# Begin the loads of one-hot matrices on ScalarE instead of SyncE, and drop the last layer's store of node rows

## The reference, cut to what matters

```python
x = x @ encW + encb
ea = edge_attr @ eencW + eencb
x = _genconv(x, src, dst, ea, ...)            # layer 0
for i in range(1, L):                         # layers 1, 2, 3
    h = relu(_ln(x, normG[i], normB[i]))
    h = _genconv(h, src, dst, ea, ...)
    x = x + h
...
# _genconv: m = relu(x[src] + ea) + EPS; logits = m * t
#   mx = segment_max(logits, dst); e = exp(logits - mx[dst])
#   agg = segment_sum(m * e / denom[dst], dst); h = agg + x; then a two-matrix network per node
```

## Time and profile before

| what | value |
|---|---|
| median of 3 runs | 11808.61 us (11800.38 to 11816.48) |
| the profiled execution's own time | 11828.1 us |
| its span | 11826.3 us |
| granted TensorE clock, mean of the span | 0.694 of full speed |
| TensorE matmuls, busy share of the span | 49% |
| VectorE, ScalarE, GpSimd, busy share | 55%, 28%, 55% |
| 16 DMA engines, mean moved | 115 GB/s |
| one-hot loads | 312, of 625 KB each |

### The profile page before, as it was taken

One profiled execution on the slowest core, in us unless ns is written; L12 is line 12 of the kernel. 1 busy time (PEld: TensorE's weight loads), 2 busy tenths in 40 slices (PEclk: granted clock), 3 DMA queues, 4 the chain that ended last, 5 costly groups with the idle time before them and its releaser, 6 DMA issues. The chain is left out here.

```text
span 11826.3 us, 107787 instructions
## 1 busy us (share of the span) xinstructions
PE 5802.2 (49%) x31762; PEld 4077.1 (34%) x31762; DVE 6551.7 (55%) x8055; ACT 3327.1 (28%) x4948; POOL 6522.0 (55%) x6157
## 2 busy tenths in 40 slices
PE   2333333343444444444444444444444447888887
PEld 2222222232333333333333333333333334444443
DVE  5666666664444444544444445444444457998897
ACT  1333333342333333333333333333223232111110
POOL 5455455535444444454544444544444446888887
PEclk6666666666666666666666666666666668999998
DMA  5344344333333333333333333333333334555555
GB/s 155 125 137 138 123 140 132 130 109 103 118 117 117 117 117 117 102 97 116 119 118 118 117 118 106 95 117 118 117 117 117 117 112 94 99 97 99 96 94 86
DMA packets 840467, 1354.58 MB, mean 115 GB/s; under 512 B 499934, under 2 KB 556476, under 8 KB 838730
## 3 DMA queue, kind: packets, MB, share of 16 engines
q1 hardware_dynamic: 523832, 1135.94, 27.5%
q0 software_dynamic: 312640, 214.30, 12.9%
q10 hardware_dynamic: 3916, 3.40, 0.1%
HBM read 806.66 MB, written 546.46 MB: 114 GB/s over the span
## 5 line engine op out<-in xcount | busy, mean ns | idle before, releaser
L826 POOL DMA_INDIRECT xg<-h_tab,idx x4656 | 4461.7, 958 | 4370.0 <-DVE idx L1159 2909.3
L917 PE MATMUL turn<-hb,hot 125*128 125x192 bf16 x12480 | 1872.5, 295 | 3018.0 <-issue 2977.7
L917 PEld LDWEIGHTS turn<-hb,hot 125*128 125x128 fp8e4 x12480 | 1310.6, 114 | 3571.7 <-issue 3536.0
L1159 DVE COPY idx<-idx_full 128x24 int32 x208 | 36.6, 176 | 3526.7 <-ACT zl L1035 3526.7
L933 PE MATMUL turn<-ident,sums 128*128 128x128 f32 x5184 | 1073.7, 375 | 1533.8 <-ACT st_all L1050 1140.4
L1524 POOL DMA_INDIRECT acc<-vm,tgt x1026 | 1602.9, 1562 | 341.2 <-issue 288.1
L933 PEld LDWEIGHTS turn<-ident,sums 128*128 128x128 f32 x5184 | 878.0, 222 | 1676.3 <-ACT st_all L1050 1243.6
L1066 ACT ACTIVATE hx<-turn 128x384 bf16<-128x384 f32 x156 | 76.4, 490 | 3600.9 <-PE turn L917 3553.1
L1050 ACT ACTIVATE st_all<-turn 128x512 f32<-128x512 f32 (+1 forms) x1344 | 752.3, 577 | 698.7 <-PE turn L933 321.0
L1166 DVE TENSOR_TENSOR_SCAN rx<-rp,carry,zl 128x1536 f32<-128x1536 bf16 (+1 forms) x224 | 739.9, 3303 | 360.1 <-ACT zl L1035 343.1
L1597 PE MATMUL zl<-spreadz,lo_hot 128*128 128x512 f32 x1620 | 765.5, 609 | 95.2 <-DVE spreadz L1773 95.2
(11 more groups left out here) (277 smaller groups left out, 7413.2 us busy)
## 6 DMA issues: line engine op xcount, KB each, us to landing
sums<-st_all SPq DMA_DIRECT2D x208, 1536.0 KB
hot<-hot_tab SPq DMA_DIRECT2D x312, 625.0 KB
ea<-feat SPq DMA_DIRECT2D x158, 768.0 KB
srcB<-src_flat SPq DMA_DIRECT2D x108, 768.0 KB
rp<-run_pen SPq DMA_DIRECT2D x210, 384.2 KB
xg<-h_tab,idx POOLq DMA_INDIRECT x4656
hot_tab<-hot SPq DMA_DIRECT2D x104, 625.0 KB
run_head<-zeros SPq DMA_DIRECT2D x216, 192.0 KB
```

The costliest lines, as they stand in the source:

```text
L826: g_.indirect_dma_start(xg[b][:, k, h, :], None, h_tab[:, :], bass.IndirectOffsetOnAxis(ap=idx[b][:, h, k:k + 1] if small is None else idx ...
L917: ins = pe.matmul(picked[:, :, n % 2, :], hot[n][0:PN, t_, :], hb[0:PN, t_, :, :], start=t_ == 0, stop=t_ == NT - 1, skip_group_check=True)
```

## The change

The loads of one-hot matrices for window w + 1 are begun by ScalarE, right behind its copy `hx<-turn` of window w, both at once. SyncE begins only the pair of window 0 of each layer. On ScalarE the last step of the loop over pairs of windows is written out behind the loop, since its second window is the last full one and has none after it to load for. Apart from this, SyncE no longer stores the node rows after the last layer, and waits for the semaphore of the computed rows instead of the one of the stored rows.

```diff
-                    def load_hot(l, w):
+                    def load_hot(l):
                         for n in range(HOT[l]):
-                            if isinstance(w, int) and w == 0 and n == 0:
+                            if n == 0:
                                 sp.wait_ge(hot_out, out_count(l, 0))
-                            if not (isinstance(w, int) and w == 0):
-                                sp.wait_ge(hot_ps, ps_count(l, w - 1, n))
-                            sp.dma_start(hot_words[n][0:PN, :], hot_tab[n][w]).then_inc(hot_in, 16)
+                            sp.dma_start(hot_words[n][0:PN, :], hot_tab[n][0]).then_inc(hot_in, 16)
...
-                        for w in range(2):
-                            load_hot(l, w)
+                        load_hot(l)
...
-                                load_hot(l, 2 * i + 2 + b)
...
-                        for k in range(NCH):
+                        for k in range(NCH if l + 1 < L else 0):
                             sp.wait_ge(h_ok, NCH * l + k + 1)
                             store_nodes(k)
...
-                    sp.wait_ge(tab_out, 16 * NCH * L + 16)
+                    sp.wait_ge(tab_out, 16 * NCH * (L - 1) + 16)
+                    sp.wait_ge(h_ok, NCH * L)
...
                             a.activation(hx[b][:, r, :, taken, :], part[:, :, taken, :], ACT.Copy).then_inc(hx_sb, 1)
+                        if not (isinstance(w, int) and w == FULLW - 1):
+                            for n in range(HOT[l]):
+                                a.dma_start(hot_words[n][0:PN, :], hot_tab[n][w + 1]).then_inc(hot_in, 16)
...
-                        with a.Fori(0, FULL_PAIRS - 1) as i:
+                        def pair(i):
...
+                        with a.Fori(0, FULL_PAIRS - 2) as i:
+                            pair(i)
+                        pair(FULL_PAIRS - 2)
```

## The result

The changed kernel takes 11952.04 us (median of 4 runs, 11944.34 to 11960.04) against 11807.31 us of before: ratio 1.0122, 95% interval 1.0105 to 1.014. That is 145 us slower, where 101 us were forecast. The two profiled executions lie 125 us apart (spans of 11826.3 and 11951.6 us), since that of before was 19.5 us above the median of its runs.

A forecast was written before the change was run, and what follows sets the result against it. The prediction took a serial ring through GpSimd's gathers, TensorE, ScalarE and VectorE in layers 1 to 3 to bound the kernel. Terms 99 + 0 + 3 - 1.7 gave +100 us; 11808.6 + 101 = 11910 us, range 11790 to 12250.

The forecast's parts named there:

- The main term: On ScalarE between `hx` and `keep`: issuing two DMAs adds 0.65 us a window, 153 times, +99 us.
- Two signs: In the changed profile: the ring at 43.2 to 43.4 us, about 21 matmuls of `select` left when TensorE resumes.
- the ring: Layers 1 to 3, each window: index copy, gathers, `select`, `hx`, `keep`, `u`, `zl`, next index copy; 42.64 us.
- The rival by the Trainium skill's rule: On ScalarE the issue hides wholly beside copy `hx`, so no difference: 11810 us; chance 0.08.
- the "0" for the later loads: `select` starts some 2 us later, but the count of matmuls done before TensorE stops stays: 0 us.
- The first rival: In `select`, fewer matmuls precede TensorE's stop with the later start: +1.0 us a window, 12060 us; chance 0.17.
- A: Theory of the follow-up runs: two costs, 0.65 us of ScalarE issue and 0.36 us of `select` matmuls from later loads.
- B: Theory of the follow-up runs: the DMA issue on ScalarE is the whole cost.
- The faster case: In `select`, up to 7 more matmuls precede TensorE's stop: -0.53 us a window, 11730 us; chance 0.10.
- Layer beginnings: Window 1 of a layer: both loads begin together, `select` starts some 4 us later; 1 us each, +3 us.
- The last store: Behind the last layer: SyncE no longer issues the store or waits for its landing, -1.7 us.

The follow-up runs named there:

- SyncE late: The kernel of before without the last store, SyncE waiting for copy `hx` before either load: 8775.32 us, ratio 1.0001; in a later session 8774.04 us, 0.9998.
- a1_after: The changed kernel run again with nothing altered: 11951.76 us against 11831.31 us of before, ratio 1.0105.
- `keep` first: The changed kernel with `keep` of the next window put ahead of the wait for `select`: 8774.34 us, ratio to before 0.9997.

## Why the prediction was right, and where it was off

**The main term held.** It said that `keep` would go from 0.39 to about 1.04 us behind `hx`. Over all regular windows it went from 0.45 to 1.10 us (+0.65), the first gather from 7.80 to 8.45 us behind `hx` (+0.65): 153 x 0.65 = 99 us of the 145. Taking 0.37 us for a DMA on ScalarE was high, since the median is 0.294 us; what made up for it was what I had no row for: the two don't begin with `hx` but 0.15 us later, and `keep` comes 0.11 us or, at the loop's back edge, 0.44 us behind their end. Of the 0.67 us of issue some 0.34 us lies beside the copy. That the size of the term came out to the hundredth is luck: one part was too large and the others were missing.

**Two signs that came true by luck.** I said that the ring would be 43.2 to 43.4 us, and it is 43.21; that about 21 matmuls would be left behind the stop, and it is 20.7. Both were reckoned from one window of 42.6 us and 21 matmuls, but the mean of before is 42.22 us and 18.3 matmuls. With +0.65 us and an unchanged count, as forecast, the ring would have been 42.9 us and 18.3 matmuls left. What filled the gap is the term that I put at nothing.

**The rival by the Trainium skill's rule fell where TensorE stops, and held where it doesn't.** The Trainium skill's "DMA: Bandwidth & Descriptors", section "Issuing engines are not separate DMA queues", calls the issue time usually small beside the transfer. As a ratio that agrees: the loads behind `zl` took 15.7 us from issue to `select` (6213.87 to 6229.54) against 0.294 us each. In the session with 8780 us the rival's time came out too, ratio 0.9996. But where the issuing engine is the serial part of a ring, the comparison with the transfer isn't the one that counts.

**The step that was off** is the "0" for the later loads. The count ahead of the stop was taken to stay; it fell from 47.4 to 45.3, and 2.4 matmuls more came behind it: +0.36 us a window, 55 us in all. It is mostly this term that makes 145 of the 101. The first rival was right in its sign and wrong in size: it gave +1.0 us for 2 us of added distance between the first gather and `select`, so some 0.7 us for the 1.5 us that came, twice what was measured. What I argued against it holds for the larger part: the stop isn't at a fixed time, since with `select` 1.5 us later behind the first gather it came 1.8 us later too (9.1 against 7.3 us behind that gather), and 45 of 47 matmuls were done. That the lateness of the loads is the cause of these 2.4 matmuls is argued, not shown; the three kernels that would have parted A from B (behind `keep`, SyncE late, behind `zl`) never ran where TensorE stops. The windows of the two traces of the changed kernel support half of it: from window to window the count ahead of the stop falls by 1.8 and by 2.0 matmuls per us of distance between the first gather and `select` (standard error 0.4; distances of mostly 4.0 to 4.5 us), and between the kernels it fell by 2.1 for 1.5 us. The count behind the stop shows no clear slope within a trace, and in before the distance hardly varies. The granted clock doesn't look like the cause: it was 0.81 over the matmuls ahead of the stop, 0.89 in before, but within each trace the windows with a lower clock get slightly more matmuls through, not fewer (in after 45.7 on average with a clock of 0.6 to 0.8, 44.7 above).

**The faster case** needed more matmuls ahead of the stop; there were fewer.

**Layer beginnings** were put at +3 us. From the first to the last of the 52 copies `hx` of a layer it took 2166.8 us in layer 1 before and 2201.9 us after, +35.1; layer 3 took +46.2:

```profile
L1066 ACT ACTIVATE hx<-turn x52: 490/490/490, 2688.7 to 4855.5; 128x384 bf16<-128x384 f32 x52
...
L1066 ACT ACTIVATE hx<-turn x52: 469/490/491, 7448.1 to 9606.8; 128x384 bf16<-128x384 f32 x52
```
```profile
L1063 ACT ACTIVATE hx<-turn x52: 471/491/492, 2684.1 to 4886.0; 128x384 bf16<-128x384 f32 x52
...
L1063 ACT ACTIVATE hx<-turn x52: 469/491/492, 7532.5 to 9737.4; 128x384 bf16<-128x384 f32 x52
```

51 rings of 0.99 us would be 50 us, so in these two layers the windows outside the regular order gained 15 and 4 us where I had them lose 1; in layer 2 (+55.7 us) they lost 5. The first two rings of a layer vary most: together they take 102 to 117 us, and over the three layers 330 us in before, 332 in after and 324 in its repetition. So my +3 us can't be told from what they vary by. **The last store** came as forecast, 1.5 us for 1.7 (3.2 us against 1.6 above).

Still open is what decides whether TensorE stops. It isn't TensorE alone that is held: while GpSimd's gathers of layers 1 to 3 run, SyncE's small instructions (register moves and arithmetic, waits), of 0.03 to 0.05 us as a rule, take over 0.4 us in 17% of the cases in before (484 of 2787), and in 1 of 3887 in the kernel without the last store, where TensorE doesn't stop. The register move ahead of the one-hot loads takes up to 1.5 us in before, and there never over 0.04 (ns, min/median/max):

```profile
L729 SPq MOVE hot<-hot_tab x300: 29/38/39, 1983.4 to 6559.3; - x150
```

ScalarE's and VectorE's small instructions show nothing of the kind in either condition (0 of 1489 and of 2052 in before). What TensorE and SyncE share here that the other two don't isn't shown.

Of six sessions for the experiments one had it (`a1_after`, 11831 us for before), five had not (8777 to 8780), on five chips in all: the stop was on one of them, the other four had none, one of these in two sessions. Number of kernels and presence of the changed kernel are excluded. Whether it is the chip or something that changes with time can't be told. No version was found that beats both where the stop is: `keep` first was meant to be it, and was only measured where it can't help. Nor was the other obvious one, the loads behind `keep`, measured where it could.

## What to carry to other kernels

An instruction put on an engine inside a serial ring costs its issue time in each turn, also a DMA "for free", less what runs beside the instruction ahead; look first for a place behind a long operation of that engine, where the issue lies beside it (behind `keep` the 0.67 us delayed nothing on ScalarE). Before a tenth of a microsecond per turn is argued, ask whether the ring is there in every session: the same pair of kernels differed by 1.2% and 1.0% in two sessions and by nothing in a third. Alternate windows of an unrolled loop can serve as a comparison that needs no run. And take the figures that a forecast starts from as means over many windows: one window's count of 21 hid here that the mean was 18.

## What the runs showed of the hardware

- The same kernel takes 11.8 ms or 8.78 ms, each repeated within 0.2%, by session. Where it is 11.8 ms, TensorE takes about 47 of 80 ready matmuls of `select` and then all but stops until 4.9 us behind the start of the last gather; where it is 8.78 ms it takes the 80 in 6.8 to 9.7 us (median 8.4), beside the same gathers. The gathers themselves are 0.96 us each (median), 1.26 us apart, in both.
- SyncE is held where TensorE is: 17% of its small instructions take over 0.4 us during the gathers, in before, in the changed kernel and in its repetition alike.
- The tables of the DMA queues in the profile of before (with the stop) and of the kernel without the last store (without it) both have 36 and 43 packets of the kind "instruction", and so give no hint of what TensorE waits for.
- A DMA on ScalarE takes 0.294 us (median; 0.264 at the least), in both conditions, and part of it runs beside the engine's copy; the operation behind two of them starts 0.11 us later, or 0.44 us where a loop's branch lies between. Begun beside a copy of 1.48 us, two of them delay the next operation by nothing.
- Loads of which the first begins anywhere from 3.2 us before to 0.7 us behind `hx` leave `select` at about 19 us behind `hx` and the ring at 27.7 us in the short condition; at 4.9 us behind, `select` comes at 21 us and the ring is 30.0 to 30.5 us.
